# Layer 3's second norm group moved into the MLP, its weight splits re-placed on VectorE, and the first group's spread keys made in halves

## The chip, the cores and the metric

The kernel runs on one core of one Trainium2 chip. The metric is the device time of one execution in microseconds (us); smaller is better. The core has five engines that run side by side and meet at semaphores: TensorE (PE), VectorE (DVE), ScalarE (ACT), GpSimd (POOL) and SyncE (SP, which issues the DMAs here).

## The reference

Four transformer-like layers run one after the other on x, 32 sequences of 64 tokens with 256 features, all in fp32. Layer 0 (two wide cross-attentions and an MLP) takes two thirds of the time and is not touched. The parts that matter are layer 1's attention and layer 3:

```python
# layer 1: 32 query heads, 8 key heads of 8 features, sequences of 128
scores = einsum('bkgld,bksd->bkgls', q, k) * scale + encoder_attention_mask
x = layer_norm(softmax(scores) @ v @ Wo + bo + hidden_state)
# layer 3: 16 heads of 16 features, sequences of 64
ln_out = layernorm(hidden_states, ln1_s, ln1_b)
x = hidden_states + attention(q, k, v of ln_out, ltor_mask) @ w_ao + b_ao      # phase 0
ln_out = layernorm(x, ln2_s, ln2_b)
x = x + attention(q of ln_out, k, v of encoder_states, cross_mask) @ w_co + b_co  # phase 1
ln_out = layernorm(x, ln3_s, ln3_b)
mlp_out = gelu(ln_out @ w1 + b1) @ w2 + b2
return x + mlp_out
```

## The kernel before

The 2048 tokens are 16 tiles of 128 tokens; four tiles are a group of 512 tokens. Every matrix product is done in three passes (`product`, L79 to L83): each operand is split into a high part, rounded to fp32r by ACT, and a low part, which DVE or POOL makes by a subtraction. So each product needs a "high" and then a "low" instruction ahead of it.

**The attention stage** (`narrow_attention`) serves layer 1 (names with `l1a_`) and layer 3 (`l3a_`). It starts with the projections of the first group: keys into PSUM banks, then queries. ACT takes the keys (`take_keys`, L1817) and "spreads" them: one copy of the keys for each of 4 or 8 heads, masked to that head's features, 128x512 each (`spread` on ACT, L1823; `part` gives the operands). For the first group the odd ones are made by DVE (L1998), after it has taken the queries (L1913). PE's first scores wait for the queries and for all these parts. Then the stage runs in slots written out by hand, one chunk of 16 heads each: in layer 3 slot s works on tile s of 32 (16 tiles in each of two phases). In slot s PE turns the exponentials of chunk s-3 (L1723), makes the scores of chunk s (L1697), turns the finished rows (L1751), makes values and the next group's projections, attends (L1740) and multiplies by the output weights. DVE takes the finished rows (L1933, L1936), adds the output to x (L1955), measures it (L76), finds the maximum of chunk s-1 (L1928) and multiplies chunk s by the mask (L1921). POOL subtracts the maximum (L1612), adds bo to x (L1608) and adds the mask's bias (L1619). In layer 1 there is no L1619 and DVE masks first.

**Norms of finished tiles.** In layer 3, two tiles at a time are normalised in the slots that follow (`normed_pair`): POOL makes the inverse deviation, ACT normalises (L1852), PE turns the pair into `bank_a` (L1770), ACT takes the high part (L1864), and DVE the low part. For phase 1, whose norm has a gain of its own that can't be folded into the weights, DVE first writes the scaled pair to an SBUF tile `whole` (L1984) and then subtracts from that (L1989). PE may use `bank_a` again once `whole` is written (`taken`, which waits on `whole_done`). This is done for phase 1's groups 0 and 1, in slots 23, 25, 27 and 29.

**Weights of the MLP.** w1 comes in four pieces. In slots 22, 24, 26 and 28 ACT makes a piece's high part at the slot's end (L1365) and DVE its low part, also at its slot's end (L1388).

**The MLP** (`dense_mlp`, `l3m_`) runs over four groups of tokens and eight chunks f of hidden features. In chunk f PE first makes chunk f+2's hidden sums (`first`), then the output sums of chunk f. So at f = 6 of group g it starts on group g+1. Groups 2 and 3 are normalised here, "late": POOL normalises four tiles (L1001), PE turns them at f = `LATE` (L1088), ACT takes the high part after chunk 6 (L1155), DVE writes `late_whole` (L1251), POOL the low part (L1022). Group 2's late norm is made during group 0 and group 3's during group 1.

Of the kernel before, what the change touches and what calls it, by code (L numbers as in the profile page):

```python
# [13 lines left out]
F32 = mybir.dt.float32  # L14
# [5 lines left out]
P = 128  # L20
# [868 lines left out]
def dense_mlp(chip, tag, function, prepared, out=None, turn=None, entry=None, late=None):  # L889
# [9 lines left out]
    with ExitStack() as stack:  # L899
# [29 lines left out]
        if late is not None:  # L929

            LATE = 5
            LATES = 2
# [30 lines left out]
        with nc.Block() as block:  # L963
            @block.gpsimd
            def _(pool):
# [21 lines left out]
                def normalise_late(n):  # L987
                    own = group_rows(n + 2)
# [20 lines left out]
                for g in range(NG):  # L1009
# [9 lines left out]
                    if late is not None and g < LATES:  # L1019
                        for c in range(CH):  # L1020
                            pool.wait_ge(late_whole_done, CH * g + c + 1)
                            pool.tensor_tensor(chip.h_lo[:, c, group_columns(g + 2)], late_whole[:, c, :],  # L1022
                                               chip.h_hi[:, c, group_columns(g + 2)].bitcast(F32), ALU.subtract).then_inc(late_lo, 1)
# [18 lines left out]
            def _(pe):  # L1042
                def first(g, f):
# [6 lines left out]
                    if late is not None and f == 0 and g >= 2:  # L1050
                        pe.wait_ge(late_lo, CH * (g - 1))
# [39 lines left out]
                def group(g, more):  # L1091
                    for f in range(FC):
# [4 lines left out]
                        if late is not None and g < LATES and f == LATE:  # L1097
                            turn_late(g)
# [29 lines left out]
            def _(act):  # L1128
# [23 lines left out]
                def take_late(n):  # L1152
                    for c in range(CH):
                        act.wait_ge(late_turned, CH * n + c + 1)
                        act.activation(chip.h_hi[:, c, group_columns(n + 2)], late_ps[:, c, :], ACT.Identity,  # L1155
# [8 lines left out]
                for f in range(FC):  # L1164
# [5 lines left out]
                    if late is not None and f == LATE + 1:  # L1170
# [12 lines left out]
                else:  # L1183
                    for g in range(1, NG):
                        for f in range(FC):
                            chunk(g, f)
                            if late is not None and g < LATES and f == LATE + 1:
# [3 lines left out]
            def _(dve):  # L1191
# [35 lines left out]
                def gather_late(n):  # L1227

                    own = group_rows(n + 2)
# [4 lines left out]
                def lows(g, done=None):  # L1234

                    for f in range(LEAD, FC):
# [7 lines left out]
                        if late is not None and g == 0 and f == 2:  # L1244
                            gather_late(1)
                        if late is not None and isinstance(g, int) and g < LATES and f == LATE + 1:
# [149 lines left out]
def narrow_attention(chip, tag, heads, kv_heads, phases, score_scale, multiply, tensors, beside=None, place=None, ending=None):  # L1396
# [85 lines left out]
    def normed_pair(s):  # L1482
# [3 lines left out]
        return t // 2 if t is not None and t % 2 == 1 and (t < TILES - NT or following and t < TILES - 2 * GT) else None  # L1486
# [16 lines left out]
    with ExitStack() as keep:  # L1503
# [36 lines left out]
        whole_done = sem("whole_done")  # L1540
        scaled_done, restored, remeasured, regathered, respread, inverted = (
# [7 lines left out]
        whole = sb("whole", [P, CH, 2 * P]) if beside else None  # L1549
# [15 lines left out]
        def part(m, g, engine_in):  # L1565
            k, h = m // PER, m % PER
            return (kb[g % 2][:, k, :, h, :], engine_in[:, k, :].rearrange("p (u f) -> p u f", f=SEQ), head_mask[:, h:h + 1])
# [4 lines left out]
        with nc.Block() as block:  # L1572
# [86 lines left out]
            def _(pe):  # L1659
# [1090 lines left out]
```

## Time and profile before

| | |
|---|---|
| median of 3 runs | 1737.33 us (1735.39 to 1738.09) |
| profiled execution, its own time | 1737.98 us |
| its span in the trace | 1736.1 us |
| mean granted clock of TensorE | 0.98 of full |
| busy share of the span: PE, DVE, ACT, POOL | 96%, 51%, 56%, 32% |

The span is what the trace covers; the profiled execution's own time is 1.9 us above it. Positions below are in us from the span's start. Layer 1's attention stage starts at 1114.9, layer 3's at 1389, the last MLP at 1638.7.

### The profile page before, as it was taken

Reading aid. Unit: us, or ns where it says so; the run is one execution under the profiler, and the core shown is the slowest. Engines: PE = TensorE matmul, PEld = TensorE weight load, DVE = VectorE, ACT = ScalarE, POOL = GpSimd, SP = SyncE. Lnnn points to the kernel's source line nnn. Section 1 sums busy time; section 2 is a strip of 40 time slices with the busy share of each in tenths; the row PEclk is TensorE's granted clock in tenths of the full one; section 3 lists DMA queues with packets and bytes.
Section 4 is the critical chain, followed back from the end, with each engine's and each line's share of the span. In section 5 each row is a group of like instructions: output and inputs, shape, how many; then the busy total and the mean of one; then the engine's idle time right before and its main releaser. Section 6 shows DMA issues by size and latency. Waiting matters only on the chain. (4 is left out here: it accounts for less than half of the span.)

```text
span 1736.1 us, 35411 instructions
## 1 busy us (share of the span) xinstructions
PE 1663.7 (96%) x14356; PEld 1432.9 (83%) x14356; DVE 890.0 (51%) x1672; ACT 972.4 (56%) x1856; POOL 560.5 (32%) x602
## 2 busy tenths in 40 slices
PE   7999999999999999999999989899989889997899
PEld 6999999999999999999999879767767567776698
DVE  6534334443354333333344465477859847777442
ACT  4545545554454455555455455477649857876454
POOL 5311000100053000010001154157754558877531
PEclk9999999999999999999999999999989989999799
DMA  5040000000000000000000010220010000001000
GB/s 172 25 125 15 10 24 24 0 24 24 25 1 25 25 1 24 24 12 12 24 24 0 1 31 1 57 51 2 2 23 1 1 7 2 2 7 38 1 18 32
DMA packets 59136, 40.05 MB, mean 23 GB/s; under 512 B 15725, under 2 KB 58263, under 8 KB 59031
## 3 DMA queue, kind: packets, MB, share of 16 engines
q1 hardware_dynamic: 57414, 37.78, 7.6%
q8 instruction: 75, 1.23, 0.3%
q10 hardware_dynamic: 1616, 0.79, 0.2%
q14 instruction: 31, 0.25, 0.0%
HBM read 36.46 MB, written 2.10 MB: 22 GB/s over the span
## 5 line engine op out<-in xcount | busy, mean ns | idle before, releaser
L641 ACT ACTIVATE l0a_q<-l0a_q_ps,l0a_head_bias 128x512 f32<-128x512 f32 x128 | 88.4, 690 | 331.0 <-PE l0a_q_ps L83 331.0
L849 DVE TENSOR_TENSOR l0a_c_lo<-l0a_c_ps,l0a_c_hi 128x512 fp32r<-128x512 f32 x64 | 44.3, 692 | 276.9 <-ACT l0a_c_hi L694 276.9
L329 POOL TENSOR_TENSOR l0a_w_lo<-l0a_raw,l0a_w_hi 128x512 fp32r<-128x512 f32 x32 | 41.7, 1305 | 446.6 <-ACT l0a_w_hi L612 446.6
L801 DVE TENSOR_TENSOR x<-l0a_o_ps,x 128x1024 f32<-128x1024 f32 x64 | 78.3, 1224 | 158.8 <-PE l0a_o_ps L83 127.5
L81 PE MATMUL l0a_v_ps<-l0a_wv_hi,ctx_hi 128*128 128x256 f32 x512 | 150.4, 294 | 0.0
L81 PE MATMUL l0a_o_ps<-l0a_wo_hi,l0a_c_hi 128*128 128x256 f32 x512 | 148.8, 291 | 0.9 <-DVE l0a_c_lo L849 0.9
L82 PE MATMUL l0a_v_ps<-l0a_wv_lo,ctx_hi 128*128 128x256 f32 x512 | 144.3, 282 | 0.0
L83 PE MATMUL l0a_v_ps<-l0a_wv_hi,ctx_lo 128*128 128x256 f32 x512 | 143.9, 281 | 0.0
L82 PE MATMUL l0a_o_ps<-l0a_wo_lo,l0a_c_hi 128*128 128x256 f32 x512 | 143.6, 281 | 0.0
L83 PE MATMUL l0a_o_ps<-l0a_wo_hi,l0a_c_lo 128*128 128x256 f32 x512 | 143.6, 280 | 0.0
L645 ACT ACTIVATE l0a_k<-l0a_kt_ps,l0a_head_bias 128x512 f32<-128x512 f32 x128 | 88.2, 689 | 63.1 <-PE l0a_kt_ps L83 62.7
L359 POOL TENSOR_TENSOR l0a_wo_lo<-l0a_raw_o,l0a_wo_hi 128x512 fp32r<-128x512 f32 x16 | 20.6, 1290 | 281.4 <-ACT l0a_wo_hi L671 281.4
L650 ACT ACTIVATE l0a_v<-l0a_v_ps 128x512 f32<-128x512 f32 x128 | 76.6, 598 | 61.1 <-PE l0a_v_ps L83 59.7
L81 PE MATMUL l0a_q_ps<-h_hi,l0a_w_hi 128*128 128x512 f32 x256 | 108.0, 422 | 0.2 <-DVE h_lo L876 0.2
L81 PE MATMUL l0a_kt_ps<-ctx_hi,l0a_w_hi 128*128 128x512 f32 x256 | 106.9, 417 | 0.0
L83 PE MATMUL l0a_q_ps<-h_hi,l0a_w_lo 128*128 128x512 f32 x256 | 101.5, 396 | 0.0
L82 PE MATMUL l0a_kt_ps<-ctx_lo,l0a_w_hi 128*128 128x512 f32 x256 | 101.3, 396 | 0.0
L82 PE MATMUL l0a_q_ps<-h_lo,l0a_w_hi 128*128 128x512 f32 x256 | 101.2, 395 | 0.0
L83 PE MATMUL l0a_kt_ps<-ctx_hi,l0a_w_lo 128*128 128x512 f32 x256 | 101.0, 394 | 0.0
L81 PEld LDWEIGHTS l0a_o_ps<-l0a_wo_hi,l0a_c_hi 128*128 128x128 f32 x512 | 96.3, 188 | 4.9 <-issue 1.2
L681 ACT ACTIVATE l0a_weight_t<-l0a_kt_ps 64x256 f32<-64x256 f32 x256 | 96.2, 376 | 6.2 <-PE l0a_kt_ps L522 3.1
L82 PEld LDWEIGHTS l0a_o_ps<-l0a_wo_lo,l0a_c_hi 128*128 128x128 f32 x512 | 96.5, 188 | 3.3
(444 smaller groups left out, 4917.8 us busy)
## 6 DMA issues: line engine op xcount, KB each, us to landing
l0a_raw_v<-in_L_xattn_wv_dram SPq DMA_DIRECT2D x16, 256.0 KB, 3.4
l0a_raw_o<-in_L_xattn_wo_dram SPq DMA_DIRECT2D x32, 128.0 KB, 2.8
l3a_room<-in_L_xattn_wo_dram SPq DMA_DIRECT2D x2, 2048.0 KB, 8.9
l0a_raw<-in_L_xattn_wq_dram SPq DMA_DIRECT2D x31, 128.0 KB, 2.3
l0a_raw<-in_L_xattn_wk_dram SPq DMA_DIRECT2D x31, 128.0 KB, 2.4
x<-in_x_dram SPq DMA_DIRECT2D x4, 512.0 KB, 7.9
l3a_room<-in_L_xattn_w_fc_dram SPq DMA_DIRECT2D x2, 1024.0 KB, 6.4
l3a_room<-in_ctx_dram SPq DMA_DIRECT2D x1, 2048.0 KB, 10.9
```

The lines of the kernel that those rows point to most:

```text
L81: pe.matmul(out, wh, mh, start=start, stop=False)
L82: pe.matmul(out, wh, ml, start=False, stop=False)
L83: return pe.matmul(out, wl, mh, start=False, stop=stop)
L329: return pool.tensor_tensor(w[p][1][:], raw[p][:], w[p][0][:].bitcast(F32), ALU.subtract)
L359: pool.tensor_tensor(wo[1][:], raw_o[:], wo[0][:].bitcast(F32), ALU.subtract).then_inc(wo_split, 1)
L641: act.activation(q[p][:], q_ps[:], ACT.Identity, bias=head_bias[p][:, 0:1]).then_inc(q_done, 1)
L645: act.activation(k[p][:, :, 0:SEQ], kt_ps[:].rearrange("p (b k) -> p b k", k=SEQ), ACT.Identity, bias=head_bias[p][:, 1:2]).then_inc(k_don ...
L650: act.activation(v[u % 2][:, p * GT // HP:(p + 1) * GT // HP, :] .rearrange("p t k -> p (t k)"), v_ps[:], ACT.Copy).then_inc(v_done, 1)
L681: last = act.activation(weight_t[p][half, :, :, b, :], kt_ps[half, p * GT // 2 * P:(p + 1) * GT // 2 * P] .rearrange("p (m b q) -> p m b q ...
L801: dve.tensor_tensor(chip.x[:, own, :], o_ps[:], chip.x[:, own, :], ALU.add).then_inc(added, 1)
L849: dve.tensor_tensor(c[p][1][:], attended[p][:], c[p][0][:].bitcast(F32), ALU.subtract).then_inc(c_lo, 1)
```

## The change

Five edits, all in the two functions above:

1. `dense_mlp` makes three late groups instead of two: group g+1 is now made late during group g, for g = 0, 1, 2. PE turns them at f = 3 of group 0 and at f = 5 of groups 1 and 2. `narrow_attention` of layer 3 stops its norms after phase 1's group 0, so slots 27 and 29 have none.
2. The two norms of phase 1 that are left are scaled in place in the PSUM bank, without `whole`, and the bank is released when the low part is done.
3. DVE's low part of a w1 piece stands in the slot after the one in which ACT makes the high part, between the measuring and the maximum.
4. The first group's spread keys are made in halves of four sequences, on both engines. PE's first scores wait for the first halves only.
5. DVE's first halves stand ahead of the queries, its second halves behind them. ACT's second halves stand ahead of its first slot.

```diff
@@ dense_mlp
-            LATE = 5
-            LATES = 2
+            LATE = (3, 5, 5)
+            LATES = 3
                 def normalise_late(n):
-                    own = group_rows(n + 2)
+                    own = group_rows(n + 1)
@@ first(g, f) on PE
-                    if late is not None and f == 0 and g >= 2:
-                        pe.wait_ge(late_lo, CH * (g - 1))
+                    if late is not None and f == 0 and g >= 1:
+                        pe.wait_ge(late_lo, CH * g)
@@ group(g, more) on PE
-                        if late is not None and g < LATES and f == LATE:
+                        if late is not None and g < LATES and f == LATE[g]:
                             turn_late(g)
@@ narrow_attention
-        return t // 2 if t is not None and t % 2 == 1 and (t < TILES - NT or following and t < TILES - 2 * GT) else None
+        return t // 2 if t is not None and t % 2 == 1 and (t < TILES - NT or following and t < TILES - 3 * GT) else None
@@ scores(s) on PE
+                    if s == 0:
+                        pe.wait_ge(first_act, len(FIRST_ACT))
+                        pe.wait_ge(first_dve, len(FIRST_DVE))
+                    if s == GS // 2 or s > 0 and s % GS == 0:
                         pe.wait_ge(parts_act, parts_by_act(g))
-                        if g == 0:
-                            pe.wait_ge(parts_dve, len(FIRST_DVE))
+                    if s == GS // 2:
+                        pe.wait_ge(parts_dve, len(FIRST_DVE))
@@ taken(n) on PE
-                    if 2 * n <= TILES - NT:
-                        pe.wait_ge(h_lo_done, n)
-                    else:
-                        pe.wait_ge(whole_done, n - (TILES - NT) // 2)
+                    pe.wait_ge(h_lo_done, n)
@@ on ACT
                 for x in range(KB):
                     take_keys(banks[x], x, 0)
                     for m in FIRST_ACT:
                         if m // PER == x:
-                            spread(m, 0)
+                            spread(m, 0, 0)
+                for m in FIRST_ACT:
+                    spread(m, 0, 1)
@@ rest_of_normed(m) on DVE
-                            last = dve.tensor_scalar(whole[:, x, :], turned_[:, x, :], gain[:, 0, x:x + 1], gain[:, 1, x:x + 1],
+                            last = dve.tensor_scalar(turned_[:, x, :], turned_[:, x, :], gain[:, 0, x:x + 1], gain[:, 1, x:x + 1],
                                                      ALU.mult, ALU.add)
@@ start of DVE
-                for n, (what, x) in enumerate([("k", x) for x in range(KB)] + [("q", x) for x in range(QB)]):
-                    if what == "q":
-                        take_queries(banks[n % 2], x, 0)
                 for m in FIRST_DVE:
                     dve.wait_ge(k_taken, m // PER + 1)
-                    out, in_, own = part(m, 0, kc)
+                    out, in_, own = part(m, 0, kc, 0)
+                    dve.tensor_scalar(out, in_, own, None, ALU.mult).then_inc(first_dve, 1)
+                for x in range(QB):
+                    take_queries(banks[(KB + x) % 2], x, 0)
+                for m in FIRST_DVE:
+                    out, in_, own = part(m, 0, kc, 1)
                     dve.tensor_scalar(out, in_, own, None, ALU.mult).then_inc(parts_dve, 1)
@@ DVE's slots
                     if added is not None:
                         add_output(added)
+                    if "vector" in extra and s > 0:
+                        extra["vector"](dve, s - 1 - CHUNKS)
                     if multiply and 0 <= s - 1 < CHUNKS:
                         find_top(s - 1)
...
-                    if "vector" in extra:
-                        extra["vector"](dve, s - CHUNKS)
```

DVE at the start of layer 1's attention stage, before; `l1a_kb` are the spread keys and `l1a_q` the queries:

```order
L1913 TENSOR_SCALAR l1a_q<-l1a_turn_proj_ps,l1a_bias_cols 128x512
L1913 TENSOR_SCALAR l1a_q<-l1a_turn_value_ps,l1a_bias_cols 128x512
L1998 TENSOR_SCALAR l1a_kb<-l1a_kc,l1a_head_mask 128x8x64 x4
L1923 SCALAR_TENSOR_TENSOR l1a_score<-l1a_score_ps,l1a_masks 128x1024
L1928 TENSOR_REDUCE l1a_top<-l1a_score 128x16
```

The same place in the changed kernel:

```order
L2003 TENSOR_SCALAR l1a_kb<-l1a_kc,l1a_head_mask 128x4x64 x4
L1922 TENSOR_SCALAR l1a_q<-l1a_turn_proj_ps,l1a_bias_cols 128x512
L1922 TENSOR_SCALAR l1a_q<-l1a_turn_value_ps,l1a_bias_cols 128x512
L2008 TENSOR_SCALAR l1a_kb<-l1a_kc,l1a_head_mask 128x4x64 x4
L1932 SCALAR_TENSOR_TENSOR l1a_score<-l1a_score_ps,l1a_masks 128x1024
```

The four copies are now eight of half the size, four of them ahead of the queries. Layer 3's start changes in the same way.

DVE in layer 3, end of slot 24 and slot 25, before; `l3w_place<-l3w_raw` is a w1 piece's low part:

```order
L1948 TENSOR_TENSOR l3a_o_t_lo<-l3a_out_ps,l3a_o_t_hi 128x256
L1963 BN_AGGR x_moments<-x_stats 128x2 x2
L1388 TENSOR_TENSOR l3w_place<-l3w_raw,l3w_place 128x512
L1933 RECIPROCAL l3a_inverse<-l3a_attn_ps 128x16
L1936 TENSOR_TENSOR l3a_rows<-l3a_attn_ps,l3a_inverse 128x256
L1955 TENSOR_TENSOR x<-l3a_out_ps,x 128x256
L76 BN_STATS x_stats<-x 128x6
L1928 TENSOR_REDUCE l3a_top<-l3a_room 128x16
L1921 TENSOR_TENSOR l3a_room<-l3a_score_ps,l3a_masks 128x1024
L1984 TENSOR_SCALAR l3a_whole<-l3a_turn_value_ps,l3w_gain 128x256 x2
L1989 TENSOR_TENSOR h_lo<-l3a_whole,h_hi 128x2x256
```

The same place in the changed kernel:

```order
L1957 TENSOR_TENSOR l3a_o_t_lo<-l3a_out_ps,l3a_o_t_hi 128x256
L1972 BN_AGGR x_moments<-x_stats 128x2 x2
L1942 RECIPROCAL l3a_inverse<-l3a_attn_ps 128x16
L1945 TENSOR_TENSOR l3a_rows<-l3a_attn_ps,l3a_inverse 128x256
L1964 TENSOR_TENSOR x<-l3a_out_ps,x 128x256
L76 BN_STATS x_stats<-x 128x6
L1388 TENSOR_TENSOR l3w_place<-l3w_raw,l3w_place 128x512
L1937 TENSOR_REDUCE l3a_top<-l3a_room 128x16
L1930 TENSOR_TENSOR l3a_room<-l3a_score_ps,l3a_masks 128x1024
L1993 TENSOR_SCALAR l3a_turn_value_ps<-l3a_turn_value_ps,l3w_gain 128x256 x2
L1997 TENSOR_TENSOR h_lo<-l3a_turn_value_ps,h_hi 128x2x256
```

The w1 part has moved behind four instructions, from the end of slot 24 into slot 25, and the norm's last two instructions read and write PSUM.

POOL in the MLP, in the changed kernel, from the second late group on (before, the program ended after the second `h_lo` with two additions to x and had no third late group):

```order
L990 TENSOR_SCALAR l3m_late_spread<-x_moments 128x4
L996 TENSOR_TENSOR l3m_late_inverse<-l3m_late_spread,minus_half 128x4
L1001 TENSOR_SCALAR l3m_late_rows<-x,x_moments,l3m_late_inverse 128x256 x4
L1013 TENSOR_TENSOR x<-x,l3w_b_row 128x1024
L1022 TENSOR_TENSOR h_lo<-l3m_late_whole,h_hi 128x512 x2
L990 TENSOR_SCALAR l3m_late_spread<-x_moments 128x4
```

A third late group is added behind these, and each `h_lo` is now that of the very next group.

## Rows read from the trace of the kernel before

**Rows 1.** Timeline, all engines, start of layer 1's attention: start, length, what, [idle, releaser].
```profile
1119.36 0.75 DVE L1913 TENSOR_SCALAR l1a_q<-l1a_turn_value_ps,l1a_bias_cols 128x512 f32<-128x512 f32 x1 [0.65 <-PE l1a_turn_value_ps L83]
1120.03 1.66 DVE L1998 TENSOR_SCALAR l1a_kb<-l1a_kc,l1a_head_mask 128x512 f32<-128x512 f32 x4
...
1121.84 1.98 PE L1697 MATMUL l1a_score_ps<-l1a_kb,l1a_q 64*64 64x512 f32 x8 [2.52 <-DVE l1a_kb L1998]
...
1123.88 1.22 DVE L1923 SCALAR_TENSOR_TENSOR l1a_score<-l1a_score_ps,l1a_masks 128x1024 f32<-128x1024 f32 x1 [2.19 <-PE l1a_score_ps L1697]
...
1126.44 1.90 POOL L1612 TENSOR_TENSOR l1a_score<-l1a_score,l1a_top 128x1024 f32<-128x1024 f32 x1 [10.36 <-DVE l1a_top L1928]
...
1128.80 1.06 ACT L1870 ACTIVATE l1a_score<-l1a_score 128x1024 f32<-128x1024 f32 x1
...
1132.53 0.66 PE L1723 MATMUL l1a_turn_value_ps<-ident,l1a_score 128*128 128x128 f32 x4
```

**Rows 2.** Windows, PE alone: stretch, length, busy (count), granted clock, DMA share, GB/s.
```profile
1127.00:1129.00 2.00, 2.00 (x10) 0.50 0.07 9
```

**Rows 3.** Groups by line: DVE's nearest copy of half the size.
```profile
L2711 DVE TENSOR_SCALAR l_weight<-l_expd,l_inv 128x256 f32<-128x256 f32 x32 | 10.2, 359 | 0.6
```

**Rows 4.** Timeline, all engines, start of layer 3's attention.
```profile
1398.12 1.66 DVE L1998 TENSOR_SCALAR l3a_room<-l3a_kc,l3a_head_mask 128x512 f32<-128x512 f32 x4
```

**Rows 5.** Timeline, DVE's maxima at the start of layer 3's slots 2 and 3.
```profile
1411.07 1.22 DVE L1928 TENSOR_REDUCE l3a_top<-l3a_room 128x16 f32<-128x1024 f32 x1 [3.19 <-POOL l3a_room L1619]
...
1417.32 1.22 DVE L1928 TENSOR_REDUCE l3a_top<-l3a_score 128x16 f32<-128x1024 f32 x1 [3.23 <-POOL l3a_score L1619]
```

**Rows 6.** Timeline, DVE's maxima at the start of slots 20, 21, 22 and 30.
```profile
1529.24 1.20 DVE L1928 TENSOR_REDUCE l3a_top<-l3a_room 128x16 f32<-128x1024 f32 x1
...
1536.29 1.20 DVE L1928 TENSOR_REDUCE l3a_top<-l3a_score 128x16 f32<-128x1024 f32 x1
...
1542.64 1.20 DVE L1928 TENSOR_REDUCE l3a_top<-l3a_room 128x16 f32<-128x1024 f32 x1
...
1608.07 1.20 DVE L1928 TENSOR_REDUCE l3a_top<-l3a_score 128x16 f32<-128x1024 f32 x1
```

**Rows 7.** Waits, slots 22 to 29: who waited for whom, total, times, longest.
```profile
PE l3a_out_ps L1751 <- DVE x L1955: 8.5, 7, 2.2
...
DVE l3w_place L1388 <- ACT l3w_place L1365: 8.2, 4, 2.6
```

**Rows 8.** Windows, all engines: length, busy of PE, PEld, DVE, ACT, POOL, clock.
```profile
1516.00:1542.64 26.64, 26.44 (x316) 21.01 (x312) 19.29 (x36) 21.70 (x41) 22.48 (x20) 1.00 0.01 2
...
1559.00:1576.00 17.00, 14.11 (x161) 11.13 (x162) 13.44 (x23) 11.50 (x22) 11.55 (x10) 1.00 0.06 17
```

**Rows 9.** Line L1989 alone: its two forms, shortest, median, longest in ns.
```profile
L1989 DVE TENSOR_TENSOR h_lo<-l3a_turn_value_ps,h_hi x8: 691/692/693, 1446.6 to 1540.4; 128x512 fp32r<-128x512 f32 x8
L1989 DVE TENSOR_TENSOR h_lo<-l3a_whole,h_hi x4: 1616/2335/2349, 1555.8 to 1605.1; 128x512 fp32r<-128x512 f32 x4
```

**Rows 10.** Timeline of POOL and of DVE in slot 25.
```profile
1571.43 2.38 POOL L1619 TENSOR_TENSOR l3a_room<-l3a_room,l3a_mask_bias 128x1024 f32<-128x1024 f32 x1
...
1572.02 2.35 DVE L1989 TENSOR_TENSOR h_lo<-l3a_whole,h_hi 128x512 fp32r<-128x512 f32 x1
```

**Rows 11.** Timeline, PE's first instruction of slot 24.
```profile
1555.94 0.63 PE L1723 MATMUL l3a_turn_value_ps<-ident,l3a_room 128*128 128x128 f32 x4 [0.27 <-DVE l3a_whole L1984]
```

**Rows 12.** Windows, PE alone, in slot 29.
```profile
1604.00:1606.00 2.00, 2.00 (x21) 0.50 0.00 0
```

**Rows 13.** Timeline, all engines, chunks 5 and 6 of the MLP's group 0.
```profile
1657.88 1.04 PE L1088 MATMUL l3m_late_ps<-ident,l3m_late_rows 128*128 128x128 f32 x8
...
1660.37 2.54 POOL L1022 TENSOR_TENSOR h_lo<-l3m_late_whole,h_hi 128x512 fp32r<-128x512 f32 x2 [9.55 <-DVE l3m_late_whole L1251]
...
1661.56 0.40 PE L81 MATMUL l3m_hidden_ps<-h_hi,l3w_place 128*128 128x512 f32 x1
```

**Rows 14.** Chain of work that ended last, merged, the MLP: start, length, what.
```profile
1658.05 0.87 PE l3m_late_ps L1088 x8
```

More of the change, by code:

```diff
@@ L1169, in _ @@
                         take_entry(0)
-                    if late is not None and f == LATE + 1:
+                    if late is not None and f == LATE[0] + 1:
                         take_late(0)
@@ L1186, in _ @@
                             chunk(g, f)
-                            if late is not None and g < LATES and f == LATE + 1:
+                            if late is not None and g < LATES and f == LATE[g] + 1:
                                 take_late(g)
@@ L1243, in lows @@
                             measure_group(f - 1)
[L1244 to L1246 removed]
+                        if late is not None and g == 0 and f in (2, 3):
+                            gather_late(f - 1)
+                        if late is not None and isinstance(g, int) and g < LATES and f == LATE[g] + 1:
                             for c in range(CH):
@@ L1563, in turned_before, with part @@
             return sum(1 for i in range(s) if normed_pair(i) is not None)
-        def part(m, g, engine_in):
+        def part(m, g, engine_in, side=None):
             k, h = m // PER, m % PER
-            return (kb[g % 2][:, k, :, h, :], engine_in[:, k, :].rearrange("p (u f) -> p u f", f=SEQ), head_mask[:, h:h + 1])
+            own = slice(0, GT * HB) if side is None else slice(side * GT * HB // 2, (side + 1) * GT * HB // 2)
+            return (kb[g % 2][:, k, own, h, :], engine_in[:, k, :].rearrange("p (u f) -> p u f", f=SEQ)[:, own, :], head_mask[:, h:h + 1])
         def pair_columns(h, m):
@@ L1816, in take_keys, with spread @@
                     act.wait_ge(k_made, g * KB + x + 1)
+                    if g == 1 and x == 0:
+                        act.wait_ge(parts_act, parts_by_act(0))
+                        act.wait_ge(parts_dve, len(FIRST_DVE))
                     act.activation(kc[:, x, :], src[:], ACT.Identity, bias=bias_cols[:, BK + x:BK + x + 1]).then_inc(k_taken, 1)
-                def spread(m, g):
+                def spread(m, g, side=None):
                     act.wait_ge(k_taken, g * KB + m // PER + 1)
-                    out, in_, own = part(m, g, kc)
-                    act.activation(out, in_, ACT.Copy, scale=own).then_inc(parts_act, 1)
+                    out, in_, own = part(m, g, kc, side)
+                    act.activation(out, in_, ACT.Copy, scale=own).then_inc(first_act if side == 0 else parts_act, 1)
                 def take_weights(c, i):
```

11 lines of the change are left out of this document (5 added, 6 removed).

## The prediction

> **What bounds the kernel now.** I read the page first: PE is busy nearly throughout, so the change can only pay where PE stands still or runs at half clock. Then the waits by stretch, to find where PE stands still near the edited lines, then the timelines there, and the windows for the clock. Four places came out.
>
> Start of layer 1's attention [rows 1, 2]. The last query is taken by 1120.11, but PE's first scores start at 1121.84, 0.15 behind DVE's four spread copies (1120.03 + 1.66 = 1121.69). PE stood still for 2.52 us, and its granted clock is 0.50 behind (1.2 GHz, the lower level). At half clock PE, now the slowest, reaches slot 3's first turn only at 1132.53.
>
> Start of layer 3's attention [rows 4, 5]. The same: the last query is taken when the copies start, 1398.12, and they last until 1399.78. What follows is not PE's: each maximum waits for POOL, by 3.19 and 3.23 us in these rows, and a slot takes 1417.32 - 1411.07 = 6.25 us, a ring of the maximum (1.22), POOL's subtraction, addition and bias, and the next maximum.
>
> Slots 22 to 29 of layer 3 [rows 6 to 10]. In slots 16 to 21 PE is full (26.44 of 26.64 us busy), and an even slot takes 7.05 us and an odd one 6.35. From slot 22 on eight slots take 1608.07 - 1542.64 = 65.43 us, 8.2 each, instead of the 53.6 of that rhythm. The waits name the reason: DVE waits 8.2 us for ACT's high part of w1 (4 times), all that stands behind it comes late, and PE waits 8.5 us for DVE's addition to x. Also, DVE's norm subtraction takes 2.34 us where its source is SBUF and 0.69 where it is PSUM. In slot 25 it ends at 1574.37, 0.56 behind POOL's bias (1573.81): it stood behind POOL. The Trainium skill says this too, in SBUF — State Buffer, "Who interferes with whom": a DVE instruction with two SBUF inputs contends with a GpSimd one that reads SBUF; the trace agrees, 2.34 against 0.69 us.
>
> The last MLP [rows 13, 14]. The chain that ended last runs over PE alone here, 570 pieces without a gap, the late turns among them: whatever is added on PE is paid in full.
>
> **The change, part by part.**
>
> (a) Layer 1's start. The halves ahead of the queries take 4 x 0.32 = 1.3 us at most (10.2 us for 32 of that size in [rows 3]; the full ones need 0.415 each), from 1117.3 on, when ACT has taken the keys. They end by 1118.6; the first query (ready at 1117.97) is taken 0.6 late, the second (1119.36) on time. ACT's four halves end before that too. So the scores start at 1120.25 instead of 1121.84: -1.6 us. DVE's second halves (1.3 us) fit in before the first scores are out (1.1 us and the semaphore), within 0.2 us. PE's gap shrinks to about 1 us. In layer 3's slots 22 to 29 PE has seven gaps of 1.2 us on average at L1751 [rows 7], and where they stand, at 1559 to 1576 for two, the clock stays at 1.00 [rows 8], so I take it that the clock stays up here. Then the path to slot 3's turn is scores 1.1, mask 1.22, maximum 1.22, POOL 1.90, exponential 1.06 and four hand-overs of 0.1: 6.9 us from the start of the scores, against 1132.53 - 1121.84 = 10.7. PE's own work there is half of 9.4 us and fits in. -3.8, of which I take 3.7. Behind it each slot hangs on the one before, so the 5.3 us are kept. If the clock falls all the same, only 1.6 is left: the bounds of (a) are -1.6 and -5.5.
>
> (b) Layer 3's start. The same move: -1.6. The POOL ring takes over from the first mask on, so the clock neither costs nor gives anything here.
>
> (c) Slots 22 to 31. With the w1 part moved, its wait is gone: ACT's high part is done 0.6 us and more before DVE comes to it. The instruction itself (0.69 when free) now stands between the measuring and the maximum. In an even-to-odd step it comes when POOL's bias is over (PE-bound slots leave POOL about 0.8 us), and PE's needs are all ahead of it (L1955) or have over 1 us of slack (L1948). So an even slot is PE's 7.05 again (22, 24, 26: 21.15). Slots 23 and 25 still have a norm, and PE now waits for the low part too: in place in PSUM the two scalings are taken as now, the subtraction 0.69. PE's wait at the next turn, 0.27 now [rows 11], grows to about 1.0 over the 6.35: 14.7 for the two. The trace has no instruction by which DVE writes PSUM: at best no slower than a write to SBUF, at worst 0.69 for each half-size scaling as for a full-size subtraction, +0.4 in each slot; I take the first, as its read side is unchanged. Slot 27 has no norm, PE needs 5.8, so the ring's 6.25 rules. Slots 28 and 29 have no projections: 6.25 each, plus 0.65 once for the w1 part, which then stands behind POOL's bias inside the ring. Sum 21.15 + 14.7 + 6.25 + 12.5 + 0.65 = 55.3 against 65.43: -10.1. Slots 30 and 31 were 12.78 and are 12.5: -0.3. PE is then idle for 1 to 2.5 us in each of slots 28 to 31, and in slot 29 the clock was at 0.50 already [rows 12]; I allow +1.1 for a half-clock stretch that delays an attend. (c) = -9.3, bounds -11 and -5.
>
> (d) The MLP's third late group: eight transposes more on PE, +0.87 [rows 14]. Its ACT, DVE and POOL work lies beside PE as the other two's does.
>
> (e) A new wait. `first(g+1, 0)` at f = 6 needs group g+1's low part, and for g = 1 and 2 PE turns that group only at f = 5. In [rows 13] the turn starts at 1657.88, the low part is done at 1660.37 + 2.54 = 1662.91, 5.03 later, and PE comes to f = 6 at 1661.56, 3.68 later. PE waits 1.35 + 0.05, twice, with the output sums of chunk 6 and all else queued behind: +2.8. For g = 0 the turn is at f = 3, two chunks of 2.8 us earlier, and there is 4 us to spare.
>
> **Sum.** -5.3 - 1.6 - 9.3 + 0.9 + 2.8 = -12.5. The profiled execution took 1737.98, so 1725.5; the median lies 0.65 below it. I say 1725.
>
> **The rivals.**
>
> R1, the clock falls at layer 1's start in spite of the shorter gap. For it: PE also stands for 2 us shortly before the stage's first matmul. Against: full clock with gaps of 1.2 in [rows 8]. Result 1725 + 3.7 = 1729. The Trainium skill, TensorE: Matmul & The Clock Gate, "HAM oscillation — how this bites in real kernels", says that gaps between bursts let the throttle come back; it would make R1 likelier than I have it.
>
> R2, the end of layer 3's attention gives back less: DVE's PSUM writes are slow, the w1 part stands behind POOL each time (1.65 more in three slots, as 2.34 against 0.69), or PE at half clock binds slots 28 to 31. (c) is then -5: 1729.5; with R1 1733.
>
> R3, no new wait in the MLP, because the chain in (e) runs faster or PE is already late: 1722. Against it: 5.03 against 3.68 come from one and the same group.
>
> R4, the other side. Without DVE's stalls PE outruns POOL from slot 26 on, its idle shares grow, and the clock stays at 0.50 through slots 27 to 31. Their PE work, 5.8, 5.6, 4.4, 5.6 and 4.4, doubles to 51.6 us against 37 now. Then (c) is -4.6 + 14.6 = +10, and the whole is +6.8: 1744. It decides once 12.5 us more of PE work on the path run at half clock than in the forecast. Against it: slots 2 to 6 of layer 3 have the same 6.25 rhythm without such a collapse.
>
> **Chances.** Forecast 0.60 (its own range 1722.5 to 1727.5), R1 0.13, R2 0.13 with or without R1, R3 0.10, R4 0.04. The range of 8 in 10 takes in R3, R1 and R2 alone: 1721 to 1731. A change of 0.2%, 3.5 us, is what a measurement of this kernel can tell from none. Faster 0.94, same 0.03, slower 0.03.
>
> **What would show it.** L1697 of layer 1 within 1 us of the last query, and clock 1.00 in the 10 us behind; the first maximum of layer 3 waiting for POOL as now; no wait of L1388 on L1365, and the steps between maxima near 7.05, 7.4 and 6.25; PE waiting twice for `h_lo` L1022 for 1.4 us each, near f = 6 of groups 1 and 2. The prediction is wrong if a window after 1120 shows 0.50, if L1921 or L1928 in slots 22 to 29 still come 8 us apart, or if the MLP's gaps are absent.

## The result, and the profile after

The changed kernel takes 1725.71 us (median of 4 runs, 1723.18 to 1727.88), the kernel before 1736.44 on the same occasion: ratio 0.9933, 95% interval 0.9921 to 0.9946. Faster, by about 11 us; the forecast was 1725 and its range held. The profiled execution is the slowest of the four, 1727.88, with a span of 1725.6 against 1736.1.

Start of layer 1's attention, timeline of all engines (start, length, what; idle time and releaser in brackets):

```profile
1115.83 0.53 POOL L2376 MEMSET l3a_room<- 128x512 f32 x1 [19.21 <-POOLq L65]
...
1118.26 1.14 DVE L2003 TENSOR_SCALAR l1a_kb<-l1a_kc,l1a_head_mask 128x256 f32<-128x256 f32 x4 [3.37 <-ACT l1a_kc L1824]
...
1120.34 0.75 DVE L1922 TENSOR_SCALAR l1a_q<-l1a_turn_value_ps,l1a_bias_cols 128x512 f32<-128x512 f32 x1 [0.27 <-PE l1a_turn_value_ps L83]
...
1121.14 1.09 PE L1703 MATMUL l1a_score_ps<-l1a_kb,l1a_q 64*64 64x512 f32 x8 [0.84 <-DVE l1a_q L1922]
...
1127.90 0.66 PE L1726 MATMUL l1a_turn_value_ps<-ident,l1a_score 128*128 128x128 f32 x4 [0.59 <-ACT l1a_score L1877]
1128.60 0.72 ACT L1830 ACTIVATE l1a_kb<-l1a_kc,l1a_head_mask 128x512 f32<-128x512 f32 x1
...
1129.27 1.06 ACT L1877 ACTIVATE l1a_score<-l1a_score 128x1024 f32<-128x1024 f32 x1
...
1130.23 0.58 ACT L1834 ACTIVATE l1a_weight_t<-l1a_turn_value_ps 128x512 f32<-128x512 f32 x1
...
1131.35 0.50 PE L81 MATMUL l1a_turn_proj_ps<-h_hi,l1a_wq_hi 128*128 128x512 f32 x1 [0.99 <-ACT l1a_weight_t L1834]
```

This execution reaches the stage later than the other did, so times are read from POOL's MEMSET at its start (1114.85 before, 1115.83 here). The scores start at +5.31 instead of +6.99 [rows 1], the turn of slot 3 at +12.07 instead of +17.68. PE stands still for 0.84 us instead of 2.52, and the clock behind it stays up. Windows of PE alone (stretch, length, busy, granted clock, DMA share, GB/s), which answer to [rows 2]:

```profile
1122.00:1132.00 10.00, 8.27 (x57) 1.00 0.49 145
```

Slots 22 to 30 of layer 3, DVE's maxima, as in [rows 6]:

```profile
1537.66 1.20 DVE L1937 TENSOR_REDUCE l3a_top<-l3a_room 128x16 f32<-128x1024 f32 x1
1545.31 1.21 DVE L1937 TENSOR_REDUCE l3a_top<-l3a_room 128x16 f32<-128x1024 f32 x1
1552.35 1.20 DVE L1937 TENSOR_REDUCE l3a_top<-l3a_score 128x16 f32<-128x1024 f32 x1
...
1566.94 1.20 DVE L1937 TENSOR_REDUCE l3a_top<-l3a_room 128x16 f32<-128x1024 f32 x1
...
1580.72 1.22 DVE L1937 TENSOR_REDUCE l3a_top<-l3a_room 128x16 f32<-128x1024 f32 x1 [1.11 <-POOL l3a_room L1621]
...
1593.68 1.22 DVE L1937 TENSOR_REDUCE l3a_top<-l3a_score 128x16 f32<-128x1024 f32 x1 [1.56 <-POOL l3a_score L1621]
```

The eight slots take 56.02 us instead of 65.43, and the last maximum of the stage, at 1606.17 (it was at 1620.85), ends two steps of 6.25. From slot 28 on all the maxima but slot 29's wait for POOL, as at the stage's start [rows 5]. The waits of slots 22 to 32 (who for whom, total, times, longest) no longer have DVE's wait for w1's high part [rows 7]; a new one has come:

```profile
PE l3a_out_ps L81 <- DVE l3a_o_t_lo L1957: 5.4, 4, 2.4
```

All four stand in slots 29 to 32 (2.39, 0.54, 1.95 and 0.56 us), behind the norms and not between them. Where PE's time goes in the slots before, windows of PE alone show, the second pair and the third:

```profile
1552.35:1566.94 14.59, 13.49 (x160) 1.00 0.08 20
1566.94:1580.72 13.78, 13.78 (x171) 1.00 0.32 96
```

In slots 24 and 25 PE is busy for all but 1.10 us, and 1.00 of that is one wait, for the norm's low part; in slots 26 and 27 it is busy throughout. w1's low part takes 0.67 to 0.68 us in slots 23, 25 and 27, and 1.93 in slot 29, where POOL sets the pace; the step to slot 29 is the long one of the last four, 6.71.

And the norm's subtraction, by line: shortest, median, longest in ns, to be held against [rows 9]:

```profile
L1993 DVE TENSOR_SCALAR l3a_turn_value_ps<-l3a_turn_value_ps,l3w_gain x4: 542/547/553, 1549.3 to 1564.3; 128x256 f32<-128x256 f32 x4
...
L1997 DVE TENSOR_TENSOR h_lo<-l3a_turn_value_ps,h_hi x10: 690/691/693, 1441.7 to 1564.9; 128x512 fp32r<-128x512 f32 x10
```

The MLP, timeline of all engines: its first matmul, the second late group (turned in group 1), PE's first instruction behind each of the two waits, and DVE's last addition:

```profile
1624.07 0.76 PE L81 MATMUL l3m_hidden_ps<-h_hi,l3w_place 128*128 128x512 f32 x1 [2.06 <-PEq L65]
...
1666.68 1.03 PE L1088 MATMUL l3m_late_ps<-ident,l3m_late_rows 128*128 128x128 f32 x8
...
1669.16 2.52 POOL L1022 TENSOR_TENSOR h_lo<-l3m_late_whole,h_hi 128x512 fp32r<-128x512 f32 x2 [9.29 <-DVE l3m_late_whole L1251]
...
1671.83 0.47 PE L81 MATMUL l3m_hidden_ps<-h_hi,l3w_place 128*128 128x512 f32 x1 [1.32 <-POOL h_lo L1022]
...
1696.63 0.47 PE L81 MATMUL l3m_hidden_ps<-h_hi,l3w_place 128*128 128x512 f32 x1 [1.29 <-POOL h_lo L1022]
...
1721.57 1.42 DVE L1268 TENSOR_TENSOR x<-l3m_out_ps,x 128x256 f32<-128x256 f32 x4 [0.84 <-PE l3m_out_ps L83]
```

The waits foreseen in (e) are there, 1.32 and 1.29 us. From first matmul to last addition is 97.50 us. In the kernel before it was 93.39:

```profile
1638.66 0.76 PE L81 MATMUL l3m_hidden_ps<-h_hi,l3w_place 128*128 128x512 f32 x1 [2.04 <-PEq L65]
...
1732.05 1.42 DVE L1268 TENSOR_TENSOR x<-l3m_out_ps,x 128x256 f32<-128x256 f32 x4 [0.85 <-PE l3m_out_ps L83]
```

The 10.5 us between the spans, by stage, each a difference of two such distances: everything ahead of layer 1's attention +0.98; layer 1's attention to its last maximum (148.97 to 144.15) -4.82; from there to layer 3's first maximum (140.97 to 139.86) -1.11; on to slot 22 -0.03; slots 22 to 29 -9.41; slots 30 and 31 -0.29; the rest to the end (115.25 to 119.43) +4.18.

### The profile page after: what moved, and what is told of

It reads as the page before. It is cut to its first block and busy times, and to the rows that moved or that the text cites. A ratio compares the mean times of both kernels' runs of the same rounds, so it can differ in the third digit from the quotient of the medians.

```text
span 1725.6 us, 35422 instructions
## 1 busy us (share of the span) xinstructions
PE 1656.1 (96%) x14356; PEld 1428.0 (83%) x14356; DVE 882.1 (51%) x1676; ACT 971.2 (56%) x1858; POOL 565.0 (33%) x602
```

## The experiments

Executions of one kernel spread here by 4 to 6 us, so each run was read twice: by its timed ratio, and by the distances above in its trace. "The stage's start" is the MEMSET; slots 22 to 29 are given in pairs, slot 22's maximum to slot 24's, and so on. The kernel before has 16.86, 16.20, 16.21, 16.16, the changed one 14.69, 14.59, 13.78, 12.96. Three runs (e1, e2, e3) each make one part of the diff in the kernel before; e11 adds the scaling in PSUM to e2.

**e1_halves_only**: the part of the diff on `spread`, `part`, `first_act`, `first_dve` and DVE's order, alone.

> The kernel before with the halves and DVE's order alone. Theory (the parts are separate, each with its price in the traces): layer 1's start gives 4.8 us and layer 3's 1.1, together -5.9, about 1730.5 against 1736.4; slots 22 to 29 still take 65.4 us and the MLP is unchanged. Rival (half of the change's gain at the starts only shows because later stages are shorter too, or the granted clock at layer 1's start is luck of one execution): less than 3 us, and a window after layer 1's first scores that shows 0.50.

Measured 1733.3 us against 1737.17, ratio 0.9970 (0.9958 to 0.9982), -5.2 by the ratio. By the trace layer 1's attention is 3.24 shorter (145.73) and the way to layer 3's first maximum 2.46 (138.51), together -5.7; slots 22 to 29 take 65.44, as expected. The gain doesn't depend on the other parts. But layer 1 gave 1.6 less than in the changed kernel, with the same instructions. The window shows why:

```profile
1117.00:1120.00 3.00, 3.00 (x9) 0.56 0.60 118
1120.00:1126.00 6.00, 5.15 (x35) 0.93 1.00 324
```

Here the clock is at half level for some 3.5 us inside the projections, at the stage's start, before any edited instruction, and the scores start at +6.88 instead of +5.31. e6_both, e8_full_ahead, e9_w1_even and e10_full_best show this stretch too (scores +6.86 to +6.87, last maximum +145.71 to +145.74); e4_late_333 and e5_w1_behind_rows don't (scores +5.32, last maximum +144.15 and +144.16), nor does the changed kernel. It is not the code that decides: e5_w1_behind_rows and e6_both are the same program up to the MLP, and one has it and the other not.

**e2_w1_only**: the `extra["vector"]` call moved, alone.

> The kernel before with the low part of w1 moved alone. Theory (two causes in slots 22 to 29: DVE's wait for ACT in the even steps and the 2.35 us subtraction from SBUF in the odd ones): the even steps fall from 8.1 to about 7.65, the odd ones hardly, -3 us, 1733. Rival 1 (DVE's wait is the whole cause): -9.7 us, 1726.7. Rival 2 (DVE's wait covers the subtraction's delay entirely, so that either alone gives nothing): 1736.

Measured 1732.21, ratio 0.9968 (0.9955 to 0.9980), -5.6 by the ratio. By the trace the pairs are 15.77, 15.01, 15.03, 14.99: 60.80, -4.63, closer to two causes than to either rival, but larger than expected (-3). The odd steps are the long ones now, 8.12 to 8.33. The 4.63 are what moving w1's part is worth, not the wait alone: the norm's subtraction, still from SBUF, comes at another moment too and takes 1.45 to 1.77 us instead of 2.33 to 2.35 (three of four; 1.62 in slot 29).

**e11_psum_w1**: the same with the scaling in place in PSUM; all four norms of slots 23 to 29 stay. One execution.

> The kernel before with w1's low part moved and the scaling in PSUM, all four norms of slots 23 to 29 kept. Theory (in the odd steps the price is the subtraction's SBUF source): the odd steps fall from 8.1 and 8.3 to 7.05, slots 22 to 29 take 58.6 us. Rival (the norm's own work on PE and ACT is the price): they stay over 8, 60.8 us.

Measured 1730.09 (before 1738.0). The pairs are 14.69, 14.60, 14.60, 14.24: 58.13, and the odd steps fell to 7.04, 7.05, 7.05 and 7.56. So the ladder is 65.43; w1's part moved, 60.80; scaling in PSUM, 58.13; norms of slots 27 and 29 out, 56.02. Its terms are -4.63, -2.67 and -2.11. All of h_lo now takes 0.69:

```profile
L1984 DVE TENSOR_TENSOR h_lo<-l3a_turn_value_ps,h_hi x5: 691/692/693, 1540.6 to 1598.9; 128x512 fp32r<-128x512 f32 x5
```

In e2_w1_only, where the source is SBUF but DVE comes to it at another time, it took less than in [rows 9], 1.47 in the median. That it hangs on what POOL does at that time is my reading; no run changes POOL alone:

```profile
L1989 DVE TENSOR_TENSOR h_lo<-l3a_whole,h_hi x4: 1451/1471/1771, 1555.3 to 1600.6; 128x512 fp32r<-128x512 f32 x4
```

**e3_late_psum**: the late groups and the scaling in PSUM, with w1's low part where it was.

> The kernel before with the late groups (LATE = (3, 5, 5), three of them) and the scaling in PSUM, w1's low part where it was. Theory of two causes: slots 23 and 25 lose about 1 us each and slots 27 and 29 about 1.8 each, -5.7 us; the MLP costs +4.2 as in the changed kernel; net -1.5, 1735. Rival 1 (DVE's wait for w1 is the whole cause): nothing in slots 22 to 29 and +4.2 in the MLP, 1740.6. Rival 2 (norms and subtraction are the whole cause): -9.7 + 4.2 = -5.5, 1731.

Measured 1735.16, ratio 0.9988 (0.9979 to 0.9997), -2.1 by the ratio. The pairs are 15.21, 15.01, 14.91, 14.33: 59.46, -5.97, and from the MLP's first matmul to the last addition are 97.8 us. Two causes again, and both rivals fall. -4.63 and -5.97 make 10.60, and together the parts gave 9.41: they overlap by 1.2.

**e4_late_333**: the changed kernel with the late turns two chunks earlier.

```diff
-            LATE = (3, 5, 5)
+            LATE = (3, 3, 3)
```

> The changed kernel with LATE = (3, 3, 3): the late turns of groups 1 and 2 two chunks earlier. Theory (PE's wait for the low part in groups 1 and 2 is what the late position costs): both waits go, -2.6 us against the changed kernel, 1723.1. Rival (POOL has not normalised the next late rows by chunk 3, or the turn's bank is taken, so that PE waits there instead): 1725 or more, with a wait of PE on the late rows or on h_lo of over 1 us.

Measured 1723.99, ratio 0.9924 (0.9910 to 0.9937). The intervals of this and the changed kernel overlap, the trace doesn't leave it open: neither wait is there, and from the MLP's first matmul to the last addition are 94.28 us:

```profile
1621.80 0.76 PE L81 MATMUL l3m_hidden_ps<-h_hi,l3w_place 128*128 128x512 f32 x1 [2.06 <-PEq L65]
...
1716.08 1.42 DVE L1268 TENSOR_TENSOR x<-l3m_out_ps,x 128x256 f32<-128x256 f32 x4 [0.85 <-PE l3m_out_ps L83]
```

That is 3.22 less than the changed kernel, the price of the two waits (1.32 and 1.29 standing still, and some 0.6 more), and 0.89 more than before, the eight transposes. Most of the 0.6 is overlap that the idle time leaves out: in the changed kernel the last matmul ahead of the first wait starts at 1670.23 and the first behind it at 1671.83, 1.60 later, where those ahead follow each other by 0.12, and the next needs 0.31 instead of 0.23. That is 1.56 for this wait, 1.53 for the other. The span shows only part of it, since 1.6 us more lie between the last addition and the end than in the others (5.6 instead of 4.0).

**e5_w1_behind_rows**: the changed kernel with w1's part behind the rows' low part.

```diff
-                    if "vector" in extra and s > 0:
-                        extra["vector"](dve, s - 1 - CHUNKS)
                     if multiply and 0 <= s - 1 < CHUNKS:
                         find_top(s - 1)
                     if s < CHUNKS:
                         mask_scores(s)
                     if done is not None:
                         rest_of_rows(done)
+                    if "vector" in extra and s > 0:
+                        extra["vector"](dve, s - 1 - CHUNKS)
```

> The changed kernel with w1's low part on DVE behind the mask and the low part of the rows instead of between measuring and maximum. Theory (in slots 23, 25 and 27 the maximum, the mask and the rows' low part all come 0.6 to 0.7 us late because of it, and PE waits 5.4 us in four slots for that low part): the even-to-odd steps fall from 7.55 to about 7.0, -2 us over slots 22 to 29, 1723.7. Rival (the instruction then delays the queries and the norm behind it, and PE's wait for h_lo grows by as much): 1725.7, the odd-to-even steps 7.05 become 7.6.

Measured 1727.24, ratio 0.9945 (0.9931 to 0.9958). The theory falls; of the rival the steps hold, but not its reason, since PE's wait for h_lo does not grow: the even steps are 7.06 and 6.96, the odd ones 7.63 and 7.64, and the pairs are 14.69, 14.60, 13.65, 12.99, those of the changed kernel within 0.13. The 0.6 that moves from one slot of a pair to the other was never lost. The theory's premise was a misreading as well: the 5.4 us of waits stand in slots 29 to 32, not where w1's part delays anything. What sets a pair is PE's own work with the norm in it (13.49 busy of 14.59 us above), and PE's wait there is the same in both (1.0 in each of slots 24 and 26):

```profile
PE l3a_turn_value_ps L1726 <- DVE h_lo L1997: 2.0, 2, 1.0
```

**e6_both**: e4 and e5 together.

> The changed kernel with both: w1's low part behind the rows' low part, and LATE = (3, 3, 3). Theory (the two places are 25 us apart and add up): -4.6 us, 1721.1. Rival (one of them does not give what it should, or PE, less busy, falls to the half clock in the last slots): 1723 or more.

Measured 1723.95, ratio 0.9927 (0.9913 to 0.9940). By the trace it has the pairs of e5 (55.96) and no wait in the MLP (93.33 from first matmul to last addition). The theory falls: it is e4 with nothing added. That these 93.33 are 0.95 less than e4's 94.28 goes with the clock and not the code: at the MLP's start it is at half level for 3.0 us here and for 5.1 in e4.

**e9_w1_even**: LATE = (3, 3, 3), and w1's part one slot later still.

```diff
-                    if "vector" in extra and s > 0:
-                        extra["vector"](dve, s - 1 - CHUNKS)
...
+                    if "vector" in extra and s > 1:
+                        extra["vector"](dve, s - 2 - CHUNKS)
```

> The changed kernel with LATE = (3, 3, 3) and w1's low part in slots 24, 26, 28 and 30, behind the rows' low part (one slot later than in the run before it). Theory (DVE stands still for 1.4 us ahead of the queries in the even slots, and only there): steps of 7.06, 7.04, 6.97, 7.05, 6.97 and three near 6.25, 53.9 us for slots 22 to 29 instead of 56.0, and 3.1 us less in the MLP: 5.2 less than the changed kernel, about 1720.5. Rival (the raw buffer comes free a slot later, its load and ACT's high part of the next piece come late and DVE or ACT waits again): steps of 8, 1724.

Measured 1719.25 (1717.5 to 1723.89), ratio 0.9892 (0.9874 to 0.9910): faster than the kernel before and than the changed one, whose interval lies above it. Neither the theory nor the rival describes slots 22 to 29: the pairs are 14.70, 14.60, 13.21, 12.95, 55.46 and not 53.9. With the two slots behind them it is 68.40, against 68.48 in e6. So the expected 2.1 us in the slots didn't come; the MLP's did (no wait of PE, 93.23 us). That e9 is timed at 4.7 less than e6 while their profiled spans are 1721.7 and 1721.9 I can't explain by the edit. In both, time goes with the mean granted clock of the execution: 1723.85 and 1723.89 at 0.984 and 1717.5 to 1719.3 at 0.988 and 0.989 for e9, 1723.95 to 1726.87 at 0.984, 1722.99 at 0.987 and 1721.95 at 0.988 for e6. But the clock does not make up the difference either: at 0.988 e9 takes 1719.2 and 1719.3, and e6 1721.95. It stays open.

**e8_full_ahead**: the kernel before with four full copies ahead of the queries, no halves.

```diff
-                for n, (what, x) in enumerate([("k", x) for x in range(KB)] + [("q", x) for x in range(QB)]):
-                    if what == "q":
-                        take_queries(banks[n % 2], x, 0)
                 for m in FIRST_DVE:
...
                     dve.tensor_scalar(out, in_, own, None, ALU.mult).then_inc(parts_dve, 1)
+                for x in range(QB):
+                    take_queries(banks[(KB + x) % 2], x, 0)
```

> The kernel before with DVE's four full spread copies ahead of the queries, no halves on either engine. Theory (what counts is that little work stands behind the last query): the copies end at 1117.3 + 1.66, the two queries follow by 1120.5, ACT's four end by 1119.9, so the scores start 1.3 us earlier than before (the halves gave 1.7) with the clock kept: some 4.3 us at layer 1 and 0.8 at layer 3, 1731.3. Rival (the halves are needed: the queries are held up by the copies, and PE, which waits for the bank of the queries or for them, starts no earlier): 1736, with the clock at 0.50.

Measured 1729.51, ratio 0.9958 (0.9945 to 0.9972). Timeline, DVE and PE:

```profile
1116.81 1.68 DVE L1995 TENSOR_SCALAR l1a_kb<-l1a_kc,l1a_head_mask 128x512 f32<-128x512 f32 x4 [4.57 <-ACT l1a_kc L1817]
1118.40 0.75 DVE L1913 TENSOR_SCALAR l1a_q<-l1a_turn_proj_ps,l1a_bias_cols 128x512 f32<-128x512 f32 x1
1119.23 0.75 DVE L1913 TENSOR_SCALAR l1a_q<-l1a_turn_value_ps,l1a_bias_cols 128x512 f32<-128x512 f32 x1
1120.04 1.09 PE L1697 MATMUL l1a_score_ps<-l1a_kb,l1a_q 64*64 64x512 f32 x8 [0.84 <-DVE l1a_q L1913]
```

By the ratio that is -7.3, more than the 3.25 and 1.62 by which the trace is shorter at the two starts; I can't assign the rest. The order alone does what order and halves did in e1: scores at +6.87, last maximum +145.72, as with the halves (e1: +6.88, +145.73). Those are both executions with the early half-clock stretch, which makes the queries late; without it I estimate from these durations that the full copies would hold the scores back by at most 0.3 us (copies from +2.43 on as in the changed kernel, 1.59 until the first query and 0.75 for each of two make +5.52 for the end of the second, which there is at +5.26). No trace shows that.

**e10_full_best**: e9 with full copies in place of the halves.

> The same as the run with w1's part in the even slots, but with the four full spread copies ahead of DVE's queries in place of the halves. Theory (only the order matters; the full copies end before the second query is ready): the scores of layer 1 start within 0.3 us of where the halves have them, and the time is that of the other within its interval, 1720.5. Rival (the halves matter where the clock is at 1.00 from the start, since the queries are then ready earlier than the copies end): 1 us or more later at each of two starts, 1722.5.

Measured 1721.55, ratio 0.9903 (0.9888 to 0.9918), and 55.57 for slots 22 to 29. The intervals of e9 and e10 overlap for the most part, and the measured time lies midway between theory and rival; the halves and their two semaphores buy nothing that these runs can tell. The rival's case, the clock at 1.00 from the stage's start, is not tested: this trace too has the early stretch (scores at +6.87).

**e12_halves_behind**: the changed kernel with DVE's first halves behind its queries. One execution.

```diff
-                for m in FIRST_DVE:
-                    dve.wait_ge(k_taken, m // PER + 1)
-                    out, in_, own = part(m, 0, kc, 0)
-                    dve.tensor_scalar(out, in_, own, None, ALU.mult).then_inc(first_dve, 1)
                 for x in range(QB):
                     take_queries(banks[(KB + x) % 2], x, 0)
+                for m in FIRST_DVE:
...
```

> The changed kernel with DVE's first halves behind the queries instead of ahead; the halves themselves stay. Theory (PE's standstill ahead of the first scores has to be short for the clock to stay): the scores start 1.1 us later, PE stands for 1.95 us, and the granted clock falls to 0.50 within the 5 us behind. Rival (a standstill below 2.5 us is short enough): the clock stays at 1.00 and only 1.1 us is lost.

Measured 1729.49 (before 1738.0). PE stands still for 1.99 us, and the clock falls behind it; timeline of PE, and windows:

```profile
1122.35 1.66 PE L1703 MATMUL l1a_score_ps<-l1a_kb,l1a_q 64*64 64x512 f32 x8 [1.99 <-DVE l1a_kb L2005]
```

```profile
1125.00:1130.00 5.00, 5.00 (x20) 0.54 0.13 22
```

The last maximum is at +149.55, 5.40 later than in the changed kernel. This execution has the early stretch too, which is worth 1.6 of it (as between e1 and the changed kernel, 145.73 and 144.15), and the later start of the scores 1.1; the other 2.7 go with the fallen clock. e3_late_psum, with the unchanged start and the same two stretches, has +149.02: the halves without the order are worth nothing at layer 1.

**e7_filler**: the kernel before with nine more matmuls on PE in the gap; they are extra work whose output the scores overwrite.

```diff
                     project(banks[n % 2], what, x, 0)
+                if tag == "l1a":
+                    wq = phases[0]["w"]["q"]
+                    for c in (0, 1, 0):
+                        product(pe, score_ps[0][:].rearrange("p h k -> p (h k)")[:, 0:512], wq[0][:, c, 0:P], wq[1][:, c, 0:P],
+                                chip_h[0][:, c, 0:GN], chip_h[1][:, c, 0:GN])
                 for s in range(SLOTS):
```

> The kernel before with nine matmuls more on PE (operands of a query projection, into layer 1's first score bank, which the scores then overwrite), placed between the last query projection and the first scores of layer 1; they are extra work, nothing else uses them. They fill the 2.5 us in which PE stands still there, and delay no instruction if they end before the spread keys. Theory (the 0.50 clock behind layer 1's start comes from that standstill): the clock stays 1.00, slot 3's first turn comes about 3.7 us earlier although the scores start as before; some of it is given back as in the changed kernel, -3 us, 1733.4. Rival (the clock would have fallen anyway, from PE's other idle time ahead of the stage, and the changed kernel keeps it for another reason): 0.50 in the window behind, 1736.4.

Measured 1734.93, ratio 0.9985 (0.9976 to 0.9994), -2.6. Timeline of the first scores and of slot 3's turn, and windows:

```profile
1120.14 1.09 PE L1697 MATMUL l1a_score_ps<-l1a_kb,l1a_q 64*64 64x512 f32 x8 [0.42 <-DVE l1a_kb L2003]
...
1126.90 0.66 PE L1723 MATMUL l1a_turn_value_ps<-ident,l1a_score 128*128 128x128 f32 x4 [0.58 <-ACT l1a_score L1875]
```

```profile
1122.00:1126.00 4.00, 4.00 (x29) 1.00 0.44 112
1126.00:1130.00 4.00, 2.61 (x20) 1.00 0.09 13
```

The scores start at +6.99, exactly as before, and with the clock kept slot 3's turn comes at +13.75 instead of +17.68 and the last maximum at +145.81 instead of +148.97. So 3.16 of the changed kernel's 4.82 come from the clock and 1.66 from the earlier start. Useless work on an engine that stood still made the kernel faster.

The 3.16 are not a fixed price. In the kernel before the half-clock stretch lasts 10 us (1121.6 to 1131.9). In e11_psum_w1, whose start is the same code, it lasts 7:

```profile
1124.00:1131.00 7.00, 7.00 (x28) 0.51 0.35 90
```

There the last maximum is at +147.62, so that the clock costs 1.81 against e7. With it as the measure the changed kernel's gain at layer 1 would be 3.5 and not 4.8.

## Why the prediction was right

The sum was -12.5 against a profiled execution; the two profiled spans differ by 10.5, the medians by 10.7. Of the 2.0 between, 0.98 is the stretch ahead of layer 1's attention, where the two programs are the same; the terms themselves miss by 1.0 together.

(a) Layer 1's start, -5.3 forecast, -4.82 measured. The start of the scores is -1.68 (forecast -1.6), slot 3's turn -5.61. The clause that failed is "Behind it each slot hangs on the one before, so the 5.3 us are kept": 0.8 is given back at once. ACT has a spread copy and an exponential ahead of slot 3's weights (to 1130.23, though PE's turn ended at 1128.6) and PE waits 0.99 for them. From slot 3's turn to the last maximum are 132.08 us here, 132.06 in e7_filler and 131.29 before. That PE, at half clock, was late enough to hide this before is my reading, and e12_halves_behind, with 132.29 and a fallen clock, does not fit it. That the clock falls behind the long gap and stays up behind the short one, e7 and e12 show in both directions. The size of the term has luck in it, since a stretch of 7 us, as in e11, would have left 3.5.

(b) Layer 3's start, -1.6 forecast. PE's standstill there fell from 2.51 to 0.84, -1.67; the distance from layer 1's last maximum changed by -1.11 in this execution and by -2.46 in e1_halves_only. The distance has chance in it: it is 140.97 to 141.83 in the five traces with the unchanged start, and 138.51 to 139.86 in the eight with a standstill of 0.84, with half-clock stretches of different length in between. The size is right within that.

(c) Slots 22 to 31, -9.3 forecast, -9.70 measured, with terms that missed in both directions. The steps were forecast as 7.05 and 7.35, and are 7.6 and 7.05: the pair is 14.65 and not 14.4. w1's part does delay the maximum of the odd slot by 0.6 but that doesn't matter (e5). The pair of slots 26 and 27 is 13.78 instead of 13.3: slot 27 takes POOL's 6.25 as forecast, but slot 26 takes 7.55, with w1's part ahead of slot 27's maximum. In e9, where it isn't there, the pair is 13.21, and slots 30 and 31 take the gain back (12.94 instead of 12.49). The 1.1 us allowed for the clock in slots 28 to 31 weren't needed. Taken in this order, moving w1's part was worth 4.63, the scaling in PSUM 2.67 and leaving out the two norms 2.11 (e2, e11 and the changed kernel); in another order the sizes differ, since the parts overlap by 1.2 (e3). That a scaling in place in PSUM costs no more than one into SBUF, assumed in (c), is so within some ns: 547 in the changed kernel, 541 for L1984 before.

(d) and (e), +3.7 forecast, +4.11 measured between the MLP's first matmul and the last addition: the transposes 0.89 (forecast 0.87) and the waits 3.22 (forecast 2.8, which leaves out the overlap of matmuls, see e4).

The rivals. R1 (the clock falls in spite of the shorter gap) didn't happen in any of the nine executions with a standstill of 0.85 us or less; it fell in all five with 1.99 us or more. At layer 3's start it fell within 2 us behind the first scores in five of six executions with a standstill of 1.98 to 2.52 us (not in e3_late_psum), and in none of eight with 0.84, of which four (e6, e8, e9, e10) have a half-clock stretch 13.5 us later. The rule cited for it from the Trainium skill, TensorE: Matmul & The Clock Gate, "HAM oscillation — how this bites in real kernels", that gaps between bursts let the throttle come back, is borne out by the gaps of 2 us and not by those of 0.84; its own case has longer waits than any of these. R2 falls: DVE's PSUM writes are not slow, w1's part is held up once (1.93 us, slot 29) and not in three slots, and the clock is 1.00 in slots 22 to 30. R3 falls with the rows of 1.32 and 1.29. R4 falls by the same clock (0.73 in slot 31 alone), and slots 28 to 31 take 6.25 each but for one of 6.71.

The forecast was also lucky in one respect: chance half-clock stretches, of which it knew nothing, move an execution by some 5 us, and could have carried either time away from the forecast.

## What to carry to other kernels

Where PE stands still for some 2 us ahead of a burst that then sets the pace, look at the granted clock behind it: closing the gap of 2.5 us, even with work that nothing uses, was worth 2.6 us here (interval 1.0 to 4.2; 3.2 by the trace) though the scores started no earlier. Where a step of one slot gets longer, add up the slots of a whole period before moving anything: here 0.6 us went from one slot to the next and back without a change in the sum. And where a group of work is moved to be due earlier, compare its chain with the time that the consumer needs to come there; 5.0 against 3.7 us were visible in the rows of before, and a change of one number, turning two chunks earlier, took the cost away.

## What the runs showed of the hardware that was not expected

Half-clock stretches come at the same few places in all these kernels, most of them near a standstill of PE at a stage's border, but some of them in some executions and not in others, and shorter or longer. Windows of PE early in layer 0, with the same instructions, in the changed kernel:

```profile
33.00:42.00 9.00, 6.83 (x37) 0.81 0.00 0
```

and in e5_w1_behind_rows, whose first part is the same program:

```profile
33.00:42.00 9.00, 6.83 (x50) 1.00 0.00 0
```

Of the five executions without a low clock there, four (e5, e7, e8, e10) reach layer 1's attention at 1113.07 to 1113.17 and e12 at 1114.35; the nine with one reach it at 1114.80 to 1115.91. Together with the 1.6 us at layer 1's start and a stretch of 3 or 6 us at the MLP's (clock 0.84 over its first 11 us in e6, 0.75 in the changed kernel), this would make, by my estimate, 4 to 5 us: 1.7 to 2.8 from the arrival, 1.6 at layer 1's start, 1.0 at the MLP's (94.28 against 93.33 us in e4 and e6). That is most of what runs of one kernel differ by. A difference of 2 us between two kernels is read from distances inside a stage, not from spans. Why a stretch comes in one execution and not in the next stays open.
